# First chunk of a DLRM-style kernel: Gram matrices as one small matmul for each sample on four column tiles of TensorE

## What is computed

```python
interaction = jnp.einsum('bnd,bmd->bnm', bottom_output, bottom_output)   # a 27 x 27 Gram matrix per sample
interaction_flat = interaction[:, _TRIL_R, _TRIL_C]                      # its 351 entries below the diagonal
x = jnp.concatenate([bottom_output[:, 0, :], interaction_flat, zero_pad], axis=1)   # 128 + 351 + 1 features
x = relu(x @ W0.T + b0)    # 1024
x = relu(x @ W1.T + b1)    # 1024
x = relu(x @ W2.T + b2)    # 512
x = relu(x @ W3.T + b3)    # 256
return x @ W4.T + b4       # 1
```

## Time and profile before

| | |
|---|---|
| three runs | 475.68, 476.79, 477.36 us; median 476.79 |
| the profiled execution | 477.05 us, of which the span of its instructions is 475.3 us |
| mean granted clock of TensorE | 0.996 of full |
| TensorE matmul busy | 464.9 us, 2599 instructions |
| TensorE weight loads busy | 397.1 us, 2599 instructions |
| VectorE busy | 321.1 us, 570 instructions |
| ScalarE busy | 264.6 us, 615 instructions |
| moved by DMA | 74.40 MB |

### The profile page before, as it was taken

How to read it: one execution, slowest core, us unless ns; L and a number is a source line. 1 busy time by engine, 2 the same in 40 slices (tenths; PEclk the granted TensorE clock), 3 DMA queues, 4 the chain that set the end, 5 groups by cost and what they waited for, 6 DMA issues and landing times.

```text
span 475.3 us, 7112 instructions
## 1 busy us (share of the span) xinstructions
PE 464.9 (98%) x2599; PEld 397.1 (84%) x2599; DVE 321.1 (68%) x570; ACT 264.6 (56%) x615; POOL 0.7 (0%) x6
## 2 busy tenths in 40 slices
PE   8999899999999999999999999999999999999996
PEld 8998888888888788888888878888888778899983
DVE  4698679796849878574616877765725988766244
ACT  3896477677664377555563366565553556233241
POOL 0000000000000000000000000000000000000000
PEclk9999899999999999999999999999999999999999
DMA  8998626856225630743345243653234420460100
GB/s 301 383 341 292 207 76 207 299 192 226 92 90 201 263 106 23 308 164 116 131 159 210 56 132 125 238 215 125 90 94 170 137 89 0 134 214 11 44 1 0
DMA packets 24226, 74.40 MB, mean 157 GB/s; under 512 B 3072, under 2 KB 9216, under 8 KB 20608
## 3 DMA queue, kind: packets, MB, share of 16 engines
q1 hardware_dynamic: 24192, 73.95, 44.1%
HBM read 65.55 MB, written 8.40 MB: 156 GB/s over the span
## 4 chain that ended last, share of the span: by engine, by line
PE 87%; DVE 7%; ACT 4%; issue 2%; POOLq 0%; POOL 0%; DVEq 0%
PE work L1117 16%; PE work L1119 15%; PE work L1118 15%; PE gps L1143 9%; PE acc L1117 8%; PE acc L1119 7%; PE acc L1118 7%; ACT grams L557 2%; PE gps L1129 1%; PE gps L1119 1%; PE gps L1118 1%; PE gps L1117 1%; PE work L1129 1%; PE acc L1129 1%; ACT w0h L592 1%
## 5 line engine op out<-in xcount | busy, mean ns | idle before, releaser
L541 ACT ACTIVATE grams<-gps 32x216 f32<-32x216 f32 (+1 forms) x384 | 131.4, 342 | 86.5 <-PE gps L1143 83.0
L1117 PE MATMUL work<-h1h,w1s 128*128 128x512 f32 (+1 forms) x208 | 81.1, 390 | 0.0
L1119 PE MATMUL work<-h1l,w1s 128*128 128x512 f32 (+1 forms) x208 | 80.2, 386 | 0.0
L1118 PE MATMUL work<-h1h,w1s 128*128 128x512 f32 (+1 forms) x208 | 79.3, 381 | 0.0
L1143 PEld LDWEIGHTS gps<-xs 128*123 128x123 f32 x384 | 55.3, 186 | 9.7 <-issue 2.1
L1117 PE MATMUL work<-featH,w0l 126*128 126x512 f32 (+5 forms) x160 | 57.2, 358 | 3.3 <-DVE xs L963 2.1
L1143 PE MATMUL gps<-xs 128*123 128x224 f32 x384 | 57.7, 272 | 0.0
L1118 PE MATMUL work<-featH,w0h 126*128 126x512 f32 (+5 forms) x160 | 56.3, 352 | 0.0
L751 DVE SCALAR_TENSOR_TENSOR grams<-grams 123x216 f32<-123x216 f32 x48 | 18.4, 383 | 56.2 <-ACT grams L541 56.2
L1119 PE MATMUL work<-featL,w0h 126*128 126x512 f32 (+5 forms) x160 | 56.0, 350 | 0.0
L735 DVE TENSOR_TENSOR xs<-xraw,xs 128x864 fp32r<-128x864 f32 x48 | 50.8, 1059 | 1.7
(11 more groups left out here) (124 smaller groups left out, 699.3 us busy)
## 6 DMA issues: line engine op xcount, KB each, us to landing
xraw<-x_t SPq DMA_DIRECT2D x56, 432.0 KB, 4.7
w1s<-w_parts SPq DMA_DIRECT2D x20, 1024.0 KB, 4.8
stage<-w_t SPq DMA_DIRECT2D x16, 512.0 KB, 5.7
w_parts<-w1s SPq DMA_DIRECT2D x8, 1024.0 KB, 4.9
xfirst<-x_t SPq DMA_DIRECT2D x8, 432.0 KB, 8.5
w0raw<-w_t SPq DMA_DIRECT2D x4, 512.0 KB, 9.5
w2raw<-w_t SPq DMA_DIRECT2D x4, 512.0 KB, 6.6
h1l<-w_parts SPq DMA_DIRECT2D x8, 256.0 KB, 4.0
```

What stands on the lines that cost most here:

```text
L541: last = act.activation(grams2[rows, h // 2 % 2, at:at + HALF_GROUPS, :, :], src[:, :, :, q * EVEN:q * EVEN + INPUTS], ACT.Copy)
L1117: pe.matmul(dst, wl, ah, start=start, stop=False)
L1118: pe.matmul(dst, wh, ah, start=False, stop=False)
L1119: return pe.matmul(dst, wh, al, start=False, stop=stop)
```

## The change

In the first chunk every sample's Gram matrix becomes a float32 matmul of its own, 27 stationary columns against 27 moving columns, read straight from the slice as it landed. The four samples of a group go to the four column tiles of the array and so to the four blocks of 32 partitions of PSUM. A slice's result is 128 x 216 in one PSUM bank, six banks rotate, and one activation takes the slice out. `xpad` and its copies go; eight slots named `xfirst2` lie in their place, so that with `xfirst` each of the 16 slices has its own slot and no load of this chunk waits; `xraw` is free for the next chunk. VectorE zeroes the six bank areas first. Order and counts around this move as the diff shows.

```diff
-        with nc.sbuf_tensor("xpad", [P, 2 * XSLOTS, SLICE_GROUPS * GROUP, QUAD], f32) as xpad:
+        with nc.sbuf_tensor("xfirst2", [P, FIRST_SLOTS, SCOLS], f32) as xfirst2:
             pass
...
         def first_slot(p):
-            if XSLOTS <= p < XSLOTS + FIRST_SLOTS:
-                return xfirst[:, p - XSLOTS, :]
-            return xraw[:, p % XSLOTS, :]
+            return (xfirst2 if p < FIRST_SLOTS else xfirst)[:, p % FIRST_SLOTS, :]
...
-        W0_HI_AFTER = [8, 10, 12, 14]
+        W0_HI_AFTER = [10, 12, 14, 15]
...
-        TRANSPOSE_AT = SLICES_SUB + 2
+        TRANSPOSE_AT = SLICES_SUB + 3
...
-        def first_banks(p):
-            banks = gps[:, :, :], acc[:, 0:2, :], work[:, :, :]
-            return banks[p % 3]
-        def banks_used(p):
-            return p - 3
+        FIRST_COLS = SLICE_GROUPS * INPUTS
+        def first_bank(p):
+            banks = gps[:, 0, :], gps[:, 1, :], acc[:, 0, :], acc[:, 1, :], work[:, 0, :], work[:, 1, :]
+            return banks[p % FIRST_BANKS][:, 0:FIRST_COLS]
+        FIRST_BANKS = 6
...
@@ SyncE, load_x
-                if n < XSLOTS + FIRST_SLOTS:
+                if n < SLICES:
                     sp.dma_start(first_slot(p), x_t[n, :, :]).then_inc(x_first[p], 16)
                     return
-                if n < SLICES:
-                    sp.wait_ge(xpad_done, n - XSLOTS - FIRST_SLOTS + 1)
-                elif n < SLICES + XSLOTS:
-                    sp.wait_ge(xpad_done, n - XSLOTS + 1)
-                elif p < XSLOTS:
+                if g > 1 and p < XSLOTS:
                     sp.wait_ge(gram_done, 2 * (n - XSLOTS + 1))
-                else:
+                elif p >= XSLOTS:
                     sp.wait_ge(xl_done, parts(g, p - XSLOTS))
...
@@ ScalarE, first_from_psum
-                for q in range(GROUP):
-                    rows = slice(q * QUAD, (q + 1) * QUAD)
-                    src = first_banks(p)[rows, :, 0:HALF_GROUPS * GROUP * INPUTS]
-                    src = src.rearrange("p b (g c) -> p b g c", c=GROUP * INPUTS)
-                    dst = first_grams(s)[rows, at:at + SLICE_GROUPS, :].rearrange("p (b g) n -> p b g n", b=2)
-                    last = act.activation(dst, src[:, :, :, q * INPUTS:(q + 1) * INPUTS], ACT.Copy)
-                last.then_inc(grams_out, 2)
+                act.activation(first_grams(s)[:, at:at + SLICE_GROUPS, :],
+                               first_bank(p).rearrange("p (g n) -> p g n", n=INPUTS), ACT.Copy).then_inc(grams_out, 2)
...
@@ VectorE
-            for i in range(XSLOTS):
-                dve.memset(xpad[:, 2 * i:2 * i + 2, :, INPUTS:], 0.0).then_inc(xpads_zero, 1)
+            for p in range(FIRST_BANKS):
+                dve.memset(first_bank(p), 0.0).then_inc(banks_zero, 1)
...
             def zero_pads(i):
-                dve.wait_ge(gram_done, 2 * (SLICES - 2 * (XSLOTS - 1 - i)))
+                held = min(-(-(i + 1) * 2 * SLICE_GROUPS * GROUP * QUAD // SCOLS), FIRST_SLOTS)
+                dve.wait_ge(gram_done, 2 * held)
...
-            dve.wait_ge(xpads_zero, XSLOTS)
-            for p in range(7):
-                pad_input(p)
             first_pairs(0)
-            for p in range(7, 11):
-                pad_input(p)
+            zero_pads(0)
+            zero_pads(1)
             pairs_lo_part(0, 0, True)
-            pad_input(11)
-            pad_input(12)
             first_pairs(1)
-            pad_input(13)
+            zero_pads(2)
+            zero_pads(3)
+            dense_parts(0)
             w0_lo_part(0)
             pairs_lo_part(0, 1, True)
-            pad_input(14)
+            first_pairs(2)
             w0_lo_part(1)
-            first_pairs(2)
-            pad_input(15)
-            dense_parts(0)
             w0_lo_part(2)
             pairs_lo_part(0, 2, True)
-            zero_pads(0)
+            first_pairs(3)
+            split_left(0)
             w0_lo_part(3)
...
-            split_left(0)
-            first_pairs(3)
             split_left(1)
...
-            for i in range(1, XSLOTS):
-                zero_pads(i)
...
@@ TensorE, first_gram
-                pe.wait_ge(xpad_done, p + 1)
-                ge(pe, grams_out, 2 * (banks_used(p) + 1))
+                pe.wait_ge(x_first[p], 16)
+                if p < FIRST_BANKS:
+                    pe.wait_ge(banks_zero, p + 1)
+                else:
+                    pe.wait_ge(grams_out, 2 * (p - FIRST_BANKS + 1))
+                one = first_slot(p).rearrange("p (b n) -> p b n", n=INPUTS)
                 for k in range(SLICE_GROUPS):
-                    four = xpad[:, p % (2 * XSLOTS), k * GROUP:(k + 1) * GROUP, :]
-                    at = k % HALF_GROUPS * GROUP * INPUTS
-                    last = pe.matmul(first_banks(p)[:, k // HALF_GROUPS, at:at + GROUP * INPUTS],
-                                     four.rearrange("p b n -> p (b n)"), four[:, :, 0:INPUTS], start=True, stop=True)
+                    for q in range(GROUP):
+                        b = k * GROUP + q
+                        last = pe.matmul(first_bank(p)[q * QUAD:q * QUAD + INPUTS, k * INPUTS:(k + 1) * INPUTS],
+                                         one[:, b, :], one[:, b, :], start=True, stop=True, tile_position=(0, q * QUAD))
...
@@ TensorE, layer0_left, body and the line before gram_half(1, 0, 0)
-                    pe.wait_ge(grams_out, 2 * (SLICES - 1))
+                    pe.wait_ge(grams_out, 2 * (SLICES - 4))
...
-            pe.wait_ge(pads_done, 1)
+            pe.wait_ge(pads_done, XSLOTS)
             gram_half(1, 0, 0)
...
-                if c == 0:
-                    pe.wait_ge(pads_done, XSLOTS)
```

More of the change, by code:

```diff
@@ L167, in rec_program @@
         x_in = [sem(f"x_in{i}") for i in range(XSLOTS)]
-        x_first = [sem(f"x_first{i}") for i in range(XSLOTS + FIRST_SLOTS)]
+        x_first = [sem(f"x_first{i}") for i in range(SLICES)]
         x0_in = sem("x0_in")
@@ L171, in rec_program @@
         table_in = sem("table_in")
-        xpads_zero, pads_done = sem("xpads_zero"), sem("pads_done")
+        pads_done, banks_zero = sem("pads_done"), sem("banks_zero")
         w0_hi, w0_done = sem("w0_hi"), sem("w0_done")
@@ L179, in rec_program @@
         w4_hi, w4_done = sem("w4_hi"), sem("w4_done")
-        xpad_done = sem("xpad_done")
         xh_done, xl_done = sem("xh_done"), sem("xl_done")
@@ L210, in first_slot @@
         def first_slot(p):
-            if XSLOTS <= p < XSLOTS + FIRST_SLOTS:
-                return xfirst[:, p - XSLOTS, :]
-            return xraw[:, p % XSLOTS, :]
+            return (xfirst2 if p < FIRST_SLOTS else xfirst)[:, p % FIRST_SLOTS, :]
         def loads_of_slot(g, p):
-            return SLICES // XSLOTS * (g - 1) + 1 + p // XSLOTS + 1
+            return SLICES // XSLOTS * (g - 1) + p // XSLOTS + 1
         def nth_block(i, name):
```

## The result

| | kernel before | changed kernel |
|---|---|---|
| median of four runs | 476.97 us (475.68 to 477.36) | 485.25 us (484.05 to 486.35) |
| ratio, 95% interval | | 1.0178 (1.0145 to 1.0210) |
| span of the profiled execution | 475.3 us | 484.6 us |

What follows compares the result with a forecast made beforehand. TensorE was taken as the bound, busy 464.9 of 475.3 us. Terms 0 + 0.5 - 0.4 - 3.1 - 1.5 = -4.5 us gave 472.55 from 477.05, forecast 472.3 us, range 466 to 492.

Steps and rivals of the forecast that it cites:

- Gram phase: First chunk's 16 slices: T, the time of a slice, stays 1.79 us, so 0 change, ends -4.0 and +4.2 us.
- The price of a pair: Gram matmul with its weight load, 27 by 27 columns: 24 to 32 ns, taken as 28, 64 pairs a slice.
- estimate of 25 ns for every matmul: Skill's overhead of about 60 cycles per matmul: 1.6 us a slice, a sum 3 us better; set beside the forecast.
- case of tiles side by side: DMA-bound rival in the Gram phase: pairs under 20 ns, TensorE waits for slices, 466 to 468 us; chance 0.12.
- Serial pairs: Rival: weight loads cannot run under another column tile's matmul, 57 ns a pair at least, 502 us; chance 0.17.
- issue-bound rival: Gram phase, 128 instructions a slice: 34 to 50 ns a pair, 479 to 495 us, middle about 485; chance 0.14.
- falling clock: Granted clock falling to half during the tiny matmuls; would look like the issue-bound rival, no size of its own.
- the stretch to the body: First left tile to body: 15.6 us in place of 18.7, -3.1 us, with one TensorE wait of 0.5 us.
- the clock after it: Start of the body: without the long wait before it, the 1.5 us lost at half clock go.
- -0.4 at its beginning: Layer 0 begins after 12 slices' evacuations in place of 15, so its 0.47 us wait goes.
- ScalarE and VectorE: Gram phase: one 0.35 us activation a slice, ScalarE never late; VectorE loses 16 copies, 9.7 us, memsets under 2.0 us.
- mode changes: Six switches between tiled and whole matmuls around Gram phase and transpositions: 0 to 1.0 us, taken as +0.5.

Runs made afterwards that it cites:

- whole-array kernel: Changed kernel with the whole-array matmuls of the kernel before, 16 pairs a slice, input padded in HBM without copies; 473.76 us, ratio 0.9947.
- one-tile kernel: Quiet kernel with all matmuls on column tile 0, keeping only the last of each group's four Gram matrices; 495.9 us.
- quiet kernel: Changed kernel with its Gram phase held until all slices and W0 landed, and later loads held until it is over; 492.5 us.
- hold kernel: Changed kernel with SyncE issuing the next chunk's slices and later weights only after the Gram phase; 479.26 us, ratio 1.0056.
- mixed kernel: Even slices as in the changed kernel, odd slices with two column tiles of 64 from a padded HBM layout; 477.56 us, ratio 1.0019.

## Why the prediction was wrong

**The step that failed** is the Gram phase, 16 x (T - 1.79) = 0. The forecast priced a pair by what the array takes for it, and took for granted that the pairs are there. It named the count, 32 instructions a slice becoming 128, but put it only under a rival and there as a rate of issue. What was missing is where instructions come from: they are fetched by DMA in blocks of 256, 6.2 to 6.5 us apart here beside 380 to 415 GB/s of data (6.0 in the interval in which the data ends). In the kernel before, a block is eight slices or 14 us of work, and the profile had the figure that mattered, 21 instruction transfers of 16 KB in all, in its table of DMA queues. I read that table for the data only. From the first Gram matmul to the first left tile it is 43.8 us (4.91 to 48.67) where it was 31.2 (4.76 to 35.99): 12.6 us for a term that was put at 0.

The Trainium skill, Runtime: NRT & Kernel Launch, section Instruction fetch mechanics, states the blocks of 256 instructions of 16 KiB, fetched ahead by the sequencer, and calls the cost of crossing one mostly hidden. The trace agrees on the size (16 KB, a gap every 256 instructions) and not on the cost: gaps of 2.93 to 4.76 us while data flows, and of 1.7 to 2.0 us with idle queues (0.8 where transpositions lengthen the block's work).

**The price of a pair**, 24 to 32 ns, was right for one tile (27.5) and wrong for four (8.6 at full clock, 12 at half). The estimate of 25 ns for every matmul, which the prediction set beside its sum, fits one tile and not four. The forecast's case of tiles side by side had that right, but concluded a DMA-bound phase, 466 to 468 us. With half the instructions, and half the Gram matrices, that is what happened: 468.2.

**Serial pairs** did not happen. The rule of the Trainium skill weighed there (TensorE: Matmul & The Clock Gate, Part 3, that weight loads overlap matmuls only where row groups differ) is contradicted by 9 to 12 ns a pair with the same 128 rows in all four tiles, against 27.5 on one.

**The issue-bound rival**, to which the forecast gave 0.14, names the time that was measured, about 485 us. The reason given for it, a rate of 34 to 50 ns per pair, is not what the trace shows: inside a block the pairs are at 12 ns, and 43 ns is only the mean over the gaps (43.8 us over 1024). The falling clock, which the prediction put beside it as something that would look alike, came too, but a pair at the low clock takes only 12 ns. That the time landed inside the range of 466 to 492 was luck: its reason was not in the text.

**Behind the phase** the forecast was -3.1 for the stretch to the body, -1.5 for the clock after it and -0.4 at its beginning. The clock's 1.5 us came as forecast, in the change and in the whole-array kernel. The stretch gave -1.6 in the change. Its first 4.2 us at half clock lose 1.8, and without them it would be 15.3 us, near the forecast 15.6, but behind a phase 12 us longer than the one it was worked out for. In the whole-array kernel, which has the phase that was assumed, it gave -0.9: 17.85 us measured for 15.6. There the term was mis-sized: with VectorE's block transposition in front of tile 0's split, TensorE waits twice, 2.0 us, where I had one wait of 0.5.

**ScalarE and VectorE**: one activation of 0.35 us a slice and memsets of 0.24 us, as said, and neither late in the phase. The mode changes, put at 0.5 us in all, leave no gap, and the rows allow a small cost: at full clock the next pair starts 0.48 us after three transpositions in the one-tile kernel (44.10 to 44.58) and 0.33 us after them in the whole-array kernel (19.20 to 19.53). What of these 0.15 us is the change of mode was not separated.

## What to carry to other kernels

Count instructions as a supply, not only as work: where TensorE's instructions are short, take the time in which 256 of them run, and compare it with the 3.7 us (idle queues) to 6.5 us (full queues) from block to block here. A rewrite that quadruples the instructions and shrinks each is only as fast as that, and the stretch in which all inputs are loaded is the worst place for it. Two samples per matmul, half the instructions, made the kernel 0.8% faster than before, of which 0.5% is there with whole-array matmuls too (both with the padded layout in HBM), while four tiles at 9 to 12 ns a pair lost 1.8%.

## What the runs showed of the hardware that was not expected

- TensorE's instruction blocks: 256 instructions, 3.5 to 3.7 us apart with no data moving (the quiet kernel), 6.2 to 6.5 us beside 380 to 415 GB/s (the change), and both in one execution on the two sides of 27 us (the hold kernel, 6.5 to 6.7 and 3.5 to 4.0). The block's packet comes 2.3 to 2.6 us before the restart in either case.
- Four column tiles of 32 with all 128 rows run side by side: 8.6 ns a float32 pair of 27 x 27 at full clock and 12 ns at half, in place of 27.5 on one tile.
- The granted clock fell to 0.50 in the changed kernel at 12 us, behind the first gap of 2.93 us, and stayed there until 52.9 us, and layer 0's first tiles paid for it. The two-tile matmuls pay too: 32 of them took 1.96 us in the mixed kernel's low stretch, and 1.14 before it. The record of the granted clock is not always to be trusted: in the quiet kernel it says 1.00 from 30 to 62 us, yet the three transpositions take 0.90 us there, as in the changed kernel's low stretch, and not the 0.49 us of the kernel before.
